# Register work of TensorE in the edge stage of a graph attention layer: tile addresses lowered ahead of the waits, a bit taken by a remainder

## Chip, cores and metric

One core of a Trainium2 chip runs the whole kernel in one launch. The metric is device microseconds from the start to the end of the execution.

## What is computed

The layer attends over the edges of a graph with 6250 nodes of 512 features (8 heads of 64) and 106,250 directed edges (each of 50,000 random pairs both ways, and one loop per node), sorted by destination:

```python
Q = (x @ Wq).reshape(N, H, d); K = (x @ Wk).reshape(N, H, d); V = (x @ Wv).reshape(N, H, d)
score = einsum('ehd,ehd->eh', K[src], Q[dst]) / sqrt(d)
score = exp(clip(score, -5.0, 5.0))[..., None]
wV = segment_sum(V[src] * score, dst, N)
Z = segment_sum(score, dst, N)
h = x + (wV / (Z + 1e-06)).reshape(N, D)
h = (h - mean(h, 0)) * rsqrt(var(h, 0) + 1e-05) * bn_gamma + bn_beta
return layernorm(x + h)
```

## The kernel before, in words

The program has three stages. `project` computes Q, K and V for 49 tiles of 128 nodes and stores them in HBM, K and V side by side. `attend` is the edge stage, about 1500 of the 2111 us, in which the change lies. `normalise` finishes the layer.

In the edge stage the sorted edges are cut into visits of 128 edges that belong to one tile of nodes. Two visits make a pair, and the stage walks over 440 pairs. Their buffers form a ring of 8 (`RING`): POOL fetches the rows of K and V of a pair into slot s of `kv` while seven others are at work. Each engine runs the same skeleton, `pipeline`: a few steps written out ahead, a hardware loop whose body holds 8 pairs (53 rounds), and a few steps behind. The order inside an engine is the order in which `step` is written; the engines meet at semaphores, one per slot of the ring for most.

For one pair q the engines do this:
- POOL issues two indirect DMAs (L747), one per visit, that gather 128 rows of K and V each. They wait until the slot's sums are done (`s_seg`). In every second pair it also weighs one head (L710).
- TensorE copies the rows of Q to the edges: a matmul of a one-hot matrix (`mm_sb`) with the tile of Q in `q_tile`, 2 visits × 2 halves = 4 matmuls into `q_ps` (L915). There is one `q_ps`, so the first of them waits until VectorE has multiplied the pair before (`s_mul`); the last raises `s_qx`.
- VectorE multiplies the gathered K by `q_ps` (L791), reduces it to 8 scores a row (L802), clips (L795), and weighs a part of the heads (L710). ScalarE takes the exponential (L856) and weighs 4 heads of each visit in 8 instructions (L842).
- TensorE adds the weighed rows into the sums of their nodes: 4 matmuls (8 passes in the trace) with the one-hot matrix the other way round, into one of two halves of `acc`, by the parity of the tile (L940). They wait for the weighing (`s_v`) and for the half to be emptied (`s_evict`); the last raises `s_seg`.
- In every second pair TensorE also makes the one-hot matrices of two later pairs (L925, L927), and ScalarE copies them to `mm_sb` (L852). Where a tile of nodes ends, ScalarE evicts its half of `acc` (L836, L838).

TensorE's order within a step is: q_ps of pair q + 1, the masks of q + 4 in even steps, the sums of q − 2.

Which tile a visit belongs to is data, so that TensorE and ScalarE follow it in registers. `follow` loads a mask of 16 bits per round; `bit(k)` says whether visit k starts a new tile. TensorE keeps the tile numbers of 8 visits (`tile_regs`, written at L907 and read at L932), and works out from them the parity that selects the half of `q_tile` (L915) and of `acc` (L940), and the values that `s_q` (Q's tile is loaded) and `s_evict` are compared with.
Of the kernel before, what the change touches and what calls it, by code (L numbers as in the profile page):

```python
# [25 lines left out]
F32R = mybir.dt.float32r  # L26
# [6 lines left out]
N_NODES, DIM, HEADS = 6250, 512, 8  # L33
D_HEAD = DIM // HEADS
N_EDGES = 106250
TILES = -(-N_NODES // P)
# [28 lines left out]
HALF = AGG // 2  # L65
# [9 lines left out]
def wait(eng, sem, value):  # L75

    if not (isinstance(value, int) and value <= 0):
        eng.wait_ge(sem, value)
# [547 lines left out]
def attend(nc, block, kv_d, q_d, lb_d, nb_d, xb_d, tabs, agg, rz, kv, first, x_first, s_first, s_slots, soft):  # L626
    lb, nb, q_tile, zeros, less, eps = first
    src_t, bits_row, cnt_row, ident = tabs
    with ExitStack() as ctx:
# [3 lines left out]
        def ps(name, shape, dt):  # L633
            return ctx.enter_context(nc.psum_tensor(name, shape, dt))
# [11 lines left out]
        acc = ps("acc", [P, 2, 2 * DIM], F32)  # L646
# [11 lines left out]
        s_nb, s_q = soft["s_nb"], soft["s_q"]  # L658
        s_qx, s_evc, s_evict = (soft[n] for n in ("s_qx", "s_evc", "s_evict"))
# [4 lines left out]
        def pipeline(eng, step, head):  # L664

            for q in range(-LOOKAHEAD, RING):
                step(q, q % RING, 1 + q // RING)
            with nc.Fori(1, ROUNDS - 1, engines=[eng.engine], head_slot={eng.engine: head}) as i:
                for s in range(RING):
                    step(i * RING + s, s, i + 1)  # L670
            for q in range((ROUNDS - 1) * RING, PAIRS + LAG):
                step(q, q % RING, q // RING + 1)

        def there(q):
            return not isinstance(q, int) or 0 <= q < PAIRS

        def at(s, fills, ahead):

            return (s + ahead) % RING, fills + (s + ahead) // RING

        def follow(eng, tiles):
            now, before = eng.alloc_register("mask_now"), eng.alloc_register("mask_before")
            regs = [eng.alloc_register(f"tile_{n}") for n in range(tiles)]
            for r in (now, *regs):
                eng.reg_mov(r, 0)

            def fetch(mask):
                eng.reg_mov(before, now)
                if not isinstance(mask, int) or mask < MASKS:
                    eng.reg_load(now, bits_row[0:1, bass.ds(mask, 1)])  # L690

            def bit(k, earlier=False):
                mask = eng.snap(before if earlier else now, min_val=0, max_val=2 ** VBODY - 1)
                return (mask >> k) & 1
            fetch(0)
            return regs, fetch, bit

        def one_hot(s, u, by_node):

            n = 2 * (s % 2) + u  # L700
            return mm_sb[:, s // 2, by_node, n * P:(n + 1) * P]
# [10 lines left out]
        @block.sync  # L712
        def _(sp):
            def load(t):
                sp.dma_start(q_tile[:, bass.ds(t % 2, 1), :].rearrange("p a n -> p (a n)"),
                             q_d[bass.ds(t * P, P), :]).then_inc(s_q, 16)

            sp.wait_ge(soft["s_tb"], 48)
            sp.wait_ge(soft["s_qa"], 16 * (TILES // 2 + 1))
            sp.wait_ge(soft["s_qb"], 16 * (TILES // 2))  # L720
            with sp.Fori(2, TILES) as t:
                used = sp.value_load(cnt_row[0:1, bass.ds(t - 2, 1)], min_val=1, max_val=VISITS)
                wait_apart(sp, s_qx, (used + 1) >> 1)
                sp.wait_ge(s_q, 16 * t)
                load(t)
            for t in range(FIRST_X):
                sp.dma_start(x_first[:, t, :], xb_d[t * P:(t + 1) * P, :]).then_inc(s_first, 16)
            for s in range(X_SLOTS):
                t = FIRST_X + 4 * s
                sp.wait_ge(s_seg[s], (PAIRS - 1 - s) // RING + 1)  # L730
                sp.dma_start(x_in_kv(kv, t, 4).rearrange("p (t n) -> p t n", n=DIM),
                             xb_d[t * P:(t + 4) * P, :].rearrange("(t p) n -> p t n", p=P)).then_inc(s_slots, 16)
# [147 lines left out]
        @block.tensor  # L880
        def _(pe):
            PLACES = RING
            pe.wait_ge(soft["s_visit"], 4)
            tile_regs, fetch, bit = follow(pe, PLACES)

            pe.wait_ge(soft["s_kc"], TILES // 2 + 3)
            def clear():

                pe.wait_ge(soft["s_split"], 2 * TILES)  # L890
                pe.wait_ge(soft["s_mem"], 1)
                for par in range(2):
                    for n in range(DIM - HALF, DIM + HALF, HALF // 2):
                        pe.matmul(acc[:, par, n:n + HALF // 2], zeros[:, 0:P], zeros[:, :], start=True,
                                  stop=True)
            pe.wait_ge(s_nb, 16)

            def step(q, s, fills):
                a, b, c = q + 4, q + 1, q - 2
                (sa, fa), (sb_, fb), (sc, fc) = at(s, fills, 4), at(s, fills, 1), at(s, fills, -2)  # L900
                if there(b):
                    tiles = []
                    for u in range(2):
                        v = 2 * sb_ + u
                        tile = pe.snap(pe.snap(tile_regs[(v - 1) % PLACES], min_val=0, max_val=TILES - 1)
                                       + bit(2 * s + u), min_val=0, max_val=TILES - 1)
                        pe.reg_mov(tile_regs[v % PLACES], tile)  # L907
                        tiles.append(tile)
                    multiplied = fills if isinstance(fills, int) else pe.to_reg(fills)
                    pe.wait_ge(s_mm[sb_ // 2], fb)  # L910
                    pe.wait_ge(s_q, 16 * (tiles[1] + 1))
                    for u in range(2):
                        for n in range(2):
                            part_q = q_tile[:, bass.ds(tiles[u] % 2, 1), n * DIM:(n + 1) * DIM].bitcast(F32R)
                            last = pe.matmul(q_ps[:, u, :], one_hot(sb_, u, 1), part_q, start=(n == 0),  # L915
                                             stop=(n == 1))
                            if u == n == 0 and there(q):
                                last._wait_ge(s_mul[s], multiplied)
                    last.then_inc(s_qx, 1)
                if s % 2 == 0 and there(a):  # L920
                    pe.wait_ge(s_lb[sa // LB_PAIRS], 16 * fa)
                    m1, f1 = at(s, fills, 2)
                    wait(pe, s_mm[m1 // 2], f1)
                    for n in range(4):
                        pe.matmul(mm_ps[:, 0, n * P:(n + 1) * P], lb[:, sa + n // 2, n % 2 * P:(n % 2 + 1) * P],  # L925
                                  nb[:, :], start=True, stop=True)
                    pe.matmul(mm_ps[:, 1, :], nb[:, :], lb[:, sa:sa + 2, :], start=True,  # L927
                              stop=True).then_inc(s_t[sa // 2], 1)
                if isinstance(q, int) and q == 0:
                    clear()  # L930
                if there(c):
                    tiles = [pe.snap(tile_regs[(2 * sc + u) % PLACES], min_val=0, max_val=TILES - 1)  # L932
                             for u in range(2)]
                    pe.wait_ge(s_v[sc], (2 if sc % 2 else 3) * fc)
                    pe.wait_ge(s_evict, tiles[1] + 1)
                    for u in range(2):
                        par = tiles[u] % 2
                        m = one_hot(sc, u, 0).bitcast(F32)
                        for n in range(2):
                            last = pe.matmul(acc[:, bass.ds(par, 1), DIM - (1 - n) * HALF:DIM + n * HALF], m,  # L940
                                             kv[:, sc, u, DIM + n * HALF:DIM + (n + 1) * HALF],
                                             start=False, stop=True, skip_group_check=True)
                    last.then_inc(s_seg[sc], 1)
                if s == RING - 1:
                    fetch(q // RING + 2 if isinstance(q, int) else fills + 1)
            pipeline(pe, step, PE_HEAD)

# [431 lines left out]
```

## Time and profile before

| | |
|---|---|
| median of 3 runs | 2119.94 us (2118.71 to 2123.97) |
| the profiled execution, its own time | 2113.25 us |
| its span, first to last instruction | 2111.5 us |
| granted TensorE clock, mean | 0.99 of full speed |
| TensorE matmuls busy | 1918.3 us |
| VectorE busy | 1696.9 us |
| ScalarE busy | 1377.7 us |
| POOL busy | 1249.1 us |
| share of the chain that ended last: PE, DVE, issue | 70%, 16%, 7% |

Busy times count work on data only; register steps, branches, semaphores and the issue of DMAs are not in them. PE is TensorE's matmuls, PEld its weight loads, which overlap them; a q behind an engine's name is its sequencer. The chain follows the work that ended last back to what released it. "Issue" is time in which an engine waited for nothing that the profile shows; "remote" is a releaser that the profile can't name. Ends of matmuls are modelled.

### The profile page before, as it was taken

The page shows a single profiled execution, that of the slowest core. Times are in us where ns is not written, and L with a number is a line of the kernel's source. Part 1 is how long each engine was busy: PE and PEld are TensorE (multiplying, and loading weights), DVE is VectorE, ACT ScalarE, POOL GpSimd, SP SyncE. Part 2 cuts the span into 40 slices and gives each one's busy share as a digit, 9 for nine tenths or more (in the row PEclk, how much of TensorE's full clock was granted, in tenths as well). Part 3 has the DMA queues.
Part 4 walks back from the last instruction along what each step waited for, and adds up shares of the span by engine and source line. Part 5 has one row for each costly group of instructions (what it writes and reads, how often), then busy time and mean ns, then how long its engine had stood idle before and what let it go on. Part 6 is the DMA issues. An engine that isn't in the chain of part 4 may idle for free.

```text
span 2111.5 us, 41623 instructions
## 1 busy us (share of the span) xinstructions
PE 1918.3 (91%) x7904; PEld 1351.1 (64%) x8014; DVE 1696.9 (80%) x2454; ACT 1377.7 (65%) x4602; POOL 1249.1 (59%) x1473
## 2 busy tenths in 40 slices
PE   7999999989998998998899899898899899899887
PEld 4555555547776776776677677676676677677433
DVE  6676655538888888888888888888888888888988
ACT  0001000018887887887888888788788788788866
POOL 0106663026666666666666666666666666666657
PEclk9999999999999999999999999999999999999999
DMA  4648886358998898888888989898899899889607
GB/s 172 176 147 299 293 301 237 143 206 300 315 326 291 304 322 307 313 305 309 306 307 305 325 315 311 301 314 300 296 321 309 294 317 320 307 300 331 225 0 289
DMA packets 184521, 589.09 MB, mean 279 GB/s; under 512 B 28480, under 2 KB 30240, under 8 KB 184480
## 3 DMA queue, kind: packets, MB, share of 16 engines
q0 software_dynamic: 135904, 465.14, 63.5%
q1 hardware_dynamic: 45120, 121.69, 16.2%
q10 hardware_dynamic: 3456, 1.78, 0.3%
q8 instruction: 18, 0.29, 0.1%
q14 instruction: 23, 0.19, 0.0%
HBM read 535.27 MB, written 78.91 MB: 291 GB/s over the span
## 4 chain that ended last, share of the span: by engine, by line
PE 70%; DVE 16%; issue 7%; another core or an unknown queue 2%; ACT 2%; DMA 1%; POOL 1%; SPq 0%; DVEq 0%; ACTq 0%; POOLq 0%
PE q_ps L915 26%; PE places L342 20%; PE acc L940 19%; DVE kv L791 11%; PE mm_ps L925 2%; DVE stats L1278 1%; DVE agg L1262 1%; ACT agg L1189 1%; DVE raw L802 1%; PE mm_ps L927 1%; DVE agg L1271 1%; PE places L402 1%; PE banks L1132 1%; DMA kv<-kv_d,idx 1%
## 5 line engine op out<-in xcount | busy, mean ns | idle before, releaser
L747 POOL DMA_INDIRECT kv<-kv_d,idx x880 | 891.9, 1014 | 548.9 <-issue 214.0
L842 ACT ACTIVATE kv<-kv 128x64 f32<-128x64 f32 x3520 | 888.9, 335 | 14.3
L940 PE MATMUL acc<-kv,mm_sb 128*128 128x260 f32 x3520 | 852.1, 385 | 11.9 <-issue 4.4
L940 PEld LDWEIGHTS acc<-kv,mm_sb 128*128 128x128 f32 x3520 | 672.8, 192 | 114.3 <-issue 10.7
L791 DVE TENSOR_TENSOR kv<-q_ps,kv 128x1024 f32<-128x1024 f32 x440 | 536.4, 1219 | 214.7 <-PE q_ps L915 161.1
L915 PE MATMUL q_ps<-q_tile,mm_sb 128*128 x1760 | 550.0, 434 | 146.0 <-DVE kv L791 114.7
L802 DVE TENSOR_REDUCE raw<-kv 128x16 f32<-128x1024 f32 x440 | 532.7, 1211 | 0.0
L915 PEld LDWEIGHTS q_ps<-q_tile,mm_sb 128*128 128x128 f32 x1760 | 316.9, 190 | 285.3 <-DVE kv L791 193.6
L852 ACT ACTIVATE mm_sb<-mm_ps,less 128x1024 fp32r<-128x1024 f32 x220 | 241.5, 1098 | 66.2 <-remote 60.1
L710 DVE TENSOR_TENSOR kv<-kv 128x384 f32<-128x384 f32 (+1 forms) x440 | 271.8, 618 | 0.0
L856 ACT ACTIVATE kv<-raw 128x16 f32<-128x16 f32 x440 | 92.0, 209 | 197.9 <-DVE raw L795 181.8
L342 PE MATMUL places<-t_sb,s_sb 128*128 128x512 f32 (+1 forms) x552 | 185.5, 486 | 0.0
L435 ACT COPY p<-places 128x768 f32<-128x768 f32 x23 | 18.4, 799 | 247.8 <-PE places L342 247.8
L342 PEld LDWEIGHTS places<-t_sb,s_sb 128*128 128x128 f32 x552 | 104.8, 190 | 73.6 <-issue 66.5
L710 POOL TENSOR_TENSOR kv<-kv 128x128 f32<-128x128 f32 x220 | 91.7, 417 | 60.6 <-ACT kv L856 48.5
L342 PE MATMUL places<-w_sb,x_sb 128*128 128x512 f32 (+1 forms) x368 | 126.2, 486 | 0.0
L795 DVE TENSOR_SCALAR raw<-raw 128x16 f32<-128x16 f32 x440 | 103.6, 235 | 0.0
L342 PEld LDWEIGHTS places<-w_sb,x_sb 128*128 128x128 f32 x368 | 69.8, 190 | 49.1 <-issue 44.5
L925 PEld LDWEIGHTS mm_ps<-nb,lb 128*128 128x128 bf16 x880 | 50.5, 99 | 63.2 <-issue 63.2
L925 PE MATMUL mm_ps<-nb,lb 128*128 128x128 bf16 x880 | 88.6, 224 | 1.5 <-issue 1.5
L590 DVE TENSOR_TENSOR u<-places,p 128x768 f32<-128x768 f32 x23 | 22.0, 957 | 78.3 <-PE places L342 78.3
L440 ACT COPY kv_a<-places 128x256 f32<-128x256 f32 x23 | 8.6, 372 | 98.0 <-PE places L342 55.8
(171 smaller groups left out, 1354.1 us busy)
## 6 DMA issues: line engine op xcount, KB each, us to landing
q_tile<-q_d SPq DMA_DIRECT2D x49, 512.0 KB
kv<-kv_d,idx POOLq DMA_INDIRECT x880
kv_d<-kv_a SPq DMA_DIRECT2D x25, 512.0 KB
xb<-in_x POOLq DMA_DIRECT2D x49, 256.0 KB, 4.2
xb_d<-xb POOLq DMA_DIRECT2D x49, 256.0 KB, 3.7
out_rows<-agg SPq DMA_DIRECT2D x49, 256.0 KB, 2.1
x_sb<-in_xT SPq DMA_DIRECT2D x24, 512.0 KB, 8.1
q_d<-q_a SPq DMA_DIRECT2D x24, 512.0 KB
```

What stands on the lines that cost most here:

```text
L342: last = pe.matmul(out[:, cols], left[:, c, :], right[:, c, cols], start=fresh and c == 0, stop=c == DEEP - 1, skip_group_check=True)
L710: return eng.tensor_tensor(v, v, w, ALU.mult)
L747: pool.indirect_dma_start(kv[:, s, u, 0:2 * DIM], None, kv_d, bass.IndirectOffsetOnAxis(idx[:, s, u:u + 1], 0), bounds_check=N_NODES - 1, ...
L791: dve.tensor_tensor(k, q_ps[:, :, :], k, ALU.mult).then_inc(s_mul[s], 1)
L795: dve.tensor_scalar(raw[:, s1, :, :], raw[:, s1, :, :], -5.0, 5.0, ALU.max, ALU.min).then_inc(s_clip[s1], 1)
L802: dve.tensor_reduce(raw[:, s, :, :], heads(kv[:, s, :, 0:DIM]), AX.X, ALU.add).then_inc(s_red[s], 1)
L842: return act.activation(v, v, ACT.Copy, scale=kv[:, s, u, 2 * DIM + h:2 * DIM + h + 1])
L852: act.activation(mm_sb[:, sa // 2, :, :], mm_ps[:, :, :], ACT.Relu, bias=less[:, 0:1]).then_inc(s_mm[sa // 2], 1)
L856: act.activation(kv[:, s, :, 2 * DIM:KVW], raw[:, s, :, :], ACT.Exp).then_inc(s_exp[s], 1)
L915: last = pe.matmul(q_ps[:, u, :], one_hot(sb_, u, 1), part_q, start=(n == 0), stop=(n == 1))
L925: pe.matmul(mm_ps[:, 0, n * P:(n + 1) * P], lb[:, sa + n // 2, n % 2 * P:(n % 2 + 1) * P], nb[:, :], start=True, stop=True)
L940: last = pe.matmul(acc[:, bass.ds(par, 1), DIM - (1 - n) * HALF:DIM + n * HALF], m, kv[:, sc, u, DIM + n * HALF:DIM + (n + 1) * HALF], sta ...
```

## The change

`bit` takes the lowest bit by a remainder, where it used an AND. In the q part TensorE works out the value for `s_q`, builds the four views of `q_tile` and has them lowered to register addresses (`lower_ap`) ahead of the two waits; the matmuls then use the finished views. In the part with the sums it does the same with the four views of `acc` and the value for `s_evict`. No matmul, tile or semaphore is added or taken away, and no other engine's code is touched, except that ScalarE's `bit` is the same function. Lines behind L907 move down by 5, those behind L932 by 9 (L915 is L920, L940 is L949).

```diff
--- before.py
+++ after.py
@@ -691,7 +691,7 @@
 
             def bit(k, earlier=False):
                 mask = eng.snap(before if earlier else now, min_val=0, max_val=2 ** VBODY - 1)
-                return (mask >> k) & 1
+                return (mask >> k) % 2
             fetch(0)
             return regs, fetch, bit
 
@@ -907,11 +907,16 @@
                         pe.reg_mov(tile_regs[v % PLACES], tile)
                         tiles.append(tile)
                     multiplied = fills if isinstance(fills, int) else pe.to_reg(fills)
+                    loaded = pe.snap(16 * (tiles[1] + 1), min_val=16, max_val=16 * TILES)
+                    parts = [q_tile[:, bass.ds(tiles[u] % 2, 1), n * DIM:(n + 1) * DIM].bitcast(F32R)
+                             for u in range(2) for n in range(2)]
+                    for part_q in parts:
+                        pe.lower_ap(part_q)
                     pe.wait_ge(s_mm[sb_ // 2], fb)
-                    pe.wait_ge(s_q, 16 * (tiles[1] + 1))
+                    pe.wait_ge(s_q, loaded)
                     for u in range(2):
                         for n in range(2):
-                            part_q = q_tile[:, bass.ds(tiles[u] % 2, 1), n * DIM:(n + 1) * DIM].bitcast(F32R)
+                            part_q = parts[2 * u + n]
                             last = pe.matmul(q_ps[:, u, :], one_hot(sb_, u, 1), part_q, start=(n == 0),
                                              stop=(n == 1))
                             if u == n == 0 and there(q):
@@ -931,13 +936,17 @@
                 if there(c):
                     tiles = [pe.snap(tile_regs[(2 * sc + u) % PLACES], min_val=0, max_val=TILES - 1)
                              for u in range(2)]
+                    sums = [acc[:, bass.ds(tiles[u] % 2, 1), DIM - (1 - n) * HALF:DIM + n * HALF]
+                            for u in range(2) for n in range(2)]
+                    emptied = pe.snap(tiles[1] + 1, min_val=1, max_val=TILES)
+                    for part in sums:
+                        pe.lower_ap(part)
                     pe.wait_ge(s_v[sc], (2 if sc % 2 else 3) * fc)
-                    pe.wait_ge(s_evict, tiles[1] + 1)
+                    pe.wait_ge(s_evict, emptied)
                     for u in range(2):
-                        par = tiles[u] % 2
                         m = one_hot(sc, u, 0).bitcast(F32)
                         for n in range(2):
-                            last = pe.matmul(acc[:, bass.ds(par, 1), DIM - (1 - n) * HALF:DIM + n * HALF], m,
+                            last = pe.matmul(sums[2 * u + n], m,
                                              kv[:, sc, u, DIM + n * HALF:DIM + (n + 1) * HALF],
                                              start=False, stop=True, skip_group_check=True)
                     last.then_inc(s_seg[sc], 1)
```

The q part of one pair on TensorE, before. Each row is one instruction; a row that names no operation on a tile is register work, and the brackets give the semaphores it waits for (`s_mul2` is that of slot 2):

```order
L905 ISA
L907 REGISTER_ALU
L907 ISA
L907 REGISTER_ALU
L907 ISA
L911 ISA [waits s_mm1]
L915 ISA [waits s_q]
L915 MATMUL q_ps<-q_tile,mm_sb 128x512 [waits s_mul2]
L915 ISA
L915 MATMUL q_ps<-q_tile,mm_sb 128x512
```

(The last two rows come twice more.) The same place now:

```order
L905 ISA
L907 ISA
L914 ISA x2
L916 ISA [waits s_mm1]
L920 MATMUL q_ps<-q_tile,mm_sb 128x512 [waits s_q,s_mul2]
L920 MATMUL q_ps<-q_tile,mm_sb 128x512 x3
```

Of ten register instructions five are left. Nothing stands between the matmuls, two bundles of addresses (L914) stand ahead of them, and the wait for `s_q` is a condition of the first matmul.

The sums of one pair on TensorE, right ahead of that place, before:

```order
L932 ISA
L935 REGISTER_ALU [waits s_v7]
L940 ISA [waits s_evict]
L940 MATMUL acc<-kv,mm_sb 128x260
L940 ISA
L940 MATMUL acc<-kv,mm_sb 128x260
L940 ISA
L940 MATMUL acc<-kv,mm_sb 128x260
L940 ISA
L940 MATMUL acc<-kv,mm_sb 128x260
```

and now:

```order
L937 ISA
L943 ISA x2
L945 REGISTER_ALU [waits s_v7]
L949 MATMUL acc<-kv,mm_sb 128x260 [waits s_evict]
L949 MATMUL acc<-kv,mm_sb 128x260 x3
```

Six register instructions have become four. The bundle that stood between the wait for `s_v` and the first matmul is ahead of that wait; a register step that carries the wait itself is still there.

## Rows read from the trace of the kernel before

**Rows 1.** The page, part 1: engine, busy us (share of the span), instructions.
```profile
PE 1918.3 (91%) x7904; PEld 1351.1 (64%) x8014; DVE 1696.9 (80%) x2454; ACT 1377.7 (65%) x4602; POOL 1249.1 (59%) x1473
```

**Rows 2.** Page, part 5: group, count | busy us, mean ns | idle before.
```profile
L940 PE MATMUL acc<-kv,mm_sb 128*128 128x260 f32 x3520 | 852.1, 385 | 11.9 <-issue 4.4
```

**Rows 3.** Waits, whole span: waiter <- releaser: us in total, times, longest.
```profile
POOL kv L747 <- remote: 212.7, 174, 1.7
...
DVE kv L791 <- PE q_ps L915: 161.1, 192, 1.6
...
PEld q_ps L915 <- issue: 39.8, 27, 3.1
PE q_ps L915 <- issue: 29.4, 20, 2.7
...
PEld acc L940 <- issue: 10.7, 19, 1.4
```

**Rows 4.** The chain of waits from 1707.8 to 1721.3: start us, us, what.
```profile
1707.87 1.24 DVE kv L791
...
1709.15 1.20 PE q_ps L915 x4
...
1712.56 1.89 PE q_ps L915 x4
...
1714.55 1.24 DVE kv L791
```

**Rows 5.** Timeline, 1709.8 to 1722.6: start us, us, operation [idle before].
```profile
1710.65 1.92 PE L940 MATMUL acc<-kv,mm_sb 128*128 128x260 f32 x8
...
1712.21 1.28 PE L915 MATMUL q_ps<-q_tile,mm_sb 128*128 x4
...
1712.48 0.99 POOL L747 DMA_INDIRECT kv<-kv_d,idx  x1 [0.30 <-issue]
1712.49 1.21 DVE L802 TENSOR_REDUCE raw<-kv 128x16 f32<-128x1024 f32 x1
...
1714.55 1.23 DVE L791 TENSOR_TENSOR kv<-q_ps,kv 128x1024 f32<-128x1024 f32 x1 [0.85 <-PE q_ps L915]
1715.17 1.03 POOL L747 DMA_INDIRECT kv<-kv_d,idx  x1 [1.26 <-remote]
...
1717.37 1.21 DVE L791 TENSOR_TENSOR kv<-q_ps,kv 128x1024 f32<-128x1024 f32 x1
```

**Rows 6.** Timeline from 1154 to 1160, where POOL left a hole.
```profile
1155.76 1.21 DVE L791 TENSOR_TENSOR kv<-q_ps,kv 128x1024 f32<-128x1024 f32 x1
...
1158.69 1.21 DVE L791 TENSOR_TENSOR kv<-q_ps,kv 128x1024 f32<-128x1024 f32 x1
```

**Rows 7.** TensorE's register steps of L935 and L940 at 1002.6: duration ns min/median/max.
```profile
L935 PEldq ALU_OP  x1: 36/36/36, 1002.6 to 1002.6; - x1
...
L940 PEldq FUSED_REGOPS  x1: 102/102/102, 1002.7 to 1002.7; - x1
```

**Rows 8.** Timeline from 999.9 to 1003.2: the weighings and the weight load behind them.
```profile
1000.55 2.02 ACT L842 ACTIVATE kv<-kv 128x64 f32<-128x64 f32 x8
...
1002.86 0.52 PEld L940 LDWEIGHTS acc<-kv,mm_sb 128*128 128x128 f32 x3 [0.81 <-issue]
```

**Rows 9.** Register steps of the whole span by line: count, ns min/median/max.
```profile
L907 PEldq ALU_OP  x880: 3/34/727, 461.9 to 1956.4; - x176
L907 PEldq FUSED_REGOPS  x880: 3/104/727, 462.0 to 1956.5; - x176
...
L915 PEldq FUSED_REGOPS  x1760: 3/56/724, 462.5 to 1957.8; - x196
...
L940 PEldq FUSED_REGOPS  x1760: 3/51/482, 473.8 to 1965.4; - x196
```

**Rows 10.** Register bundles of L915, 1713.9 to 1715.9: ns, first and last start.
```profile
L915 PEldq FUSED_REGOPS  x2: 13/32/51, 1714.3 to 1715.8; - x2
```

**Rows 11.** The same from 1717.5 to 1719.0.
```profile
L915 PEldq FUSED_REGOPS  x4: 51/72/105, 1717.9 to 1718.9; - x4
```

## The prediction, made before the changed kernel ran

> **What bounds the kernel now.** I read the page's busy times first: TensorE is busy for 91% of the span and VectorE for 80% [rows 1], so no engine can be named from shares alone. The costliest groups come next: beside a matmul group stands the idle time just ahead of it, and the sums by node (L940) are 852.1 us of work with 11.9 us of idle [rows 2]. So their group hardly ever stands still for its own reasons. The waits tell more. Inside the edge stage two large ones belong together: POOL's gathers wait 212.7 us for a "remote", 174 times, and VectorE's multiplication (L791) waits 161.1 us, 192 times, for the q_ps matmuls (L915) [rows 3]. TensorE in turn may not overwrite q_ps before that multiplication is over, so the two form a loop that all 440 pairs of visits run through.
>
> The chain of waits over two pairs shows it as a cycle of 6.68 us, from the multiplication at 1707.87 to that at 1714.55: multiplication 1.24, q_ps matmuls 1.20, mask matmuls, sums, and then q_ps matmuls again, which the chain prices at 1.89 us [rows 4]. The timeline of the same place gives that last group 1.28 us: it begins at 1712.21 and is over by 1713.49, VectorE's reduce by 1713.70, yet the multiplication begins at 1714.55, 0.85 us after VectorE was free and 1.06 us after the matmuls' end [rows 5]. In the same instant something else is late: POOL's gather of 1715.17 waited 1.26 us for a "remote" though the sums that it needs ended at 1712.57 (10.65 + 1.92) [rows 5]. Both late signals follow the fourth of four back-to-back gathers (1712.48). Where POOL leaves a hole between gathers, the multiplication begins without any gap: 1155.76 and 1158.69, a step of 2.93 us against 3.34 in the cycle [rows 6]. So I read the bound as this: half of the pairs lose some 0.8 us because TensorE's updates arrive late while POOL gathers, and in a pair where they do not, VectorE sets the pace.
>
> **The change, part by part.** Counted in the two orders, TensorE's sequencer runs 16 register instructions a pair before (10 for the q part, 6 for the sums) and 9 after. All are in the sequencer and none in the array, so each costs time only where the array or a waiter stands still for it.
>
> *The sums.* Before, behind the wait for the weighed rows stood the register move that carries it (36 ns), a bundle (102 ns) and a step to the first weight load [rows 7]. The one clear place: ScalarE's eight weighings end at 1002.57 (1000.55 + 2.02), the weight load begins at 1002.86 [rows 8]. Of these 0.29 us the move stays (L945 still carries the wait), the bundle goes, and with it I take half of the remaining 0.15 us of steps: 0.10 + 0.06 = 0.16 us. It is gained only where TensorE had nothing else to do: the waits name 19 such starts, 10.7 us in all [rows 3]. 19 × 0.16 = **3.0 us**. The other 421 starts follow matmuls without a hole, and what hides the bundle there is the matmuls ahead of it.
>
> *The bundles between the matmuls of a group* (3 for q_ps, 3 for the sums, medians 56 and 51 ns [rows 9]) go away. The chain has the four q_ps matmuls in 1.20 us [rows 4], 0.30 us each, five times a bundle; the cover is the array itself: 0. A page's rule bears on this. The Trainium skill, "Perfetto Trace Analysis", Sequencer Loop and Tensor Engine Instruction, has a waiting matmul pushed into a queue, with the sequencer free to go on. By that rule the register work behind a waiting matmul was hidden before as well, and the whole edit would be worth 0. The trace disagrees in one place: the bundle ahead of the first q_ps matmul ran at 1714.3 and the next only at 1715.8, when the multiplication that the matmul waits for was over [rows 10]. So the sequencer stood with the matmul, and I keep the 3.0 us, which the rule does not give.
>
> *The q part.* Here the change moves work to a dearer place: three address bundles that stood between matmuls now stand ahead of the first (3 × 56 ns), and a bit costs a remainder in place of an AND of its own. The first bundle of L940, which takes the parity of the tile by a remainder, was 102 ns long [rows 7], against a median of 51 over all four of its bundles, and an AND is a step of 34 ns [rows 9]; so + 51 ns twice, less two ANDs: 168 + 102 − 68 = **+ 0.20 us** from the last matmul of the sums to the wait for the multiplication. The cover: where TensorE had waited, the sequencer stood from 1714.3 to 1715.8, 1.4 us of slack [rows 10]. Where TensorE runs on without a hole, the sequencer comes to its wait near 1718.0, and the multiplication ends at 1718.58 (1717.37 + 1.21): 0.5 us [rows 5, 11]. Both are over 0.20, so 0. The bounds: at best the pair loses all the idle time put on "issue" ahead of this group's weight loads, 39.8 us in 27 times [rows 3]; at worst the 0.20 us stand bare in each second pair, 220 × 0.20 = 44 us. I take 0, by the two covers.
>
> *The waits on s_q and s_evict* now compare with a register worked out ahead. Neither of the two stands among TensorE's larger waits, so 0. The wait on s_q becomes a condition of the matmul, with nothing of TensorE's queued behind it that did not stand behind it before. *ScalarE* loses three of four ALU steps at L870, which at the 36 ns of TensorE's [rows 7] are 0.11 us a pair beside eight weighings of 2.02 us; ScalarE is at 65% and not in the chain: 0. VectorE, POOL, SyncE and every DMA stay as they are.
>
> **Sum**: 2113.25 us of the profiled run − 3.0 = 2110.25. That run lies 6.7 us below the median of 2119.94, so the forecast for the median is **2117 us**, less than 0.3% (6.4 us) away from no change, and that is about what a measurement of this kernel can tell from none.
>
> **Rivals.** *Faster: the late signals are TensorE's own doing.* If the q_ps update comes late because TensorE's sequencer is busy with register steps, fewer of them make it earlier. For: only signals of TensorE and POOL are late, and the steps have outliers of 727 ns against medians of 104 and less [rows 9]. Against: POOL's share in it, and the undisturbed pairs with the same register work and no gap [rows 6]. Prices: in proportion to the instructions, 7/16 of VectorE's 161.1 us = 70 us, to 2050. If only the idle time put on "issue" shrinks by that share, 29.4 us ahead of q_ps, with all 11.9 us ahead of the sums [rows 2, 3], it is 41.3 × 7/16 = 18 us, to 2102. There is also a threshold: the sums end 0.09 us after the fourth gather's start (1712.57 against 1712.48 [rows 5]), and a little less delay might let their signal through in time. I give the mild form 0.25 and the large one 0.10.
>
> The Trainium skill, "Perfetto Trace Analysis", Tensor Engine Instruction, says that the end of a matmul in the profile is an estimate and that its signal goes out when PSUM has acknowledged. By that rule alone the 1.06 us would be matmuls still running, TensorE would be the bound, and a change in its sequencer would give 0. The undisturbed pairs, whose multiplication starts with no gap behind the same matmuls, speak against it; it would alter nothing in the forecast.
>
> *Slower: the longer row of register steps ahead of the first q_ps matmul meets its wait too late.* It decides from a cover of less than 0.20 us. For: there is idle time put on "issue" ahead of this group's weight loads, 27 times, and ahead of its matmuls, 20 times [rows 3]; there the sequencer already comes last, and each would lose the full 0.20: at most 47 × 0.20 = 9 us, to 2129. If the cover of 0.5 us that I read at one place is missing in many of the pairs without a hole, up to 44 us, to 2164. Against: both covers [rows 5, 10, 11]. I give it 0.20, most of it near 2129.
>
> *The change doesn't do what it says.* In part this is so: the value that s_q is compared with is still made by the step that waits for s_mm, and L945 still follows s_v. What is left behind the wait is 36 ns; had the bundle stayed too, the 3.0 us would be 0 and the forecast 2120, which is inside it.
>
> **How the numbers follow.** Forecast (no difference to be seen) 0.45; faster 0.35; slower 0.20. The range reaches down to 2085, half of the large form's 70 us, and up to 2136, past the 9 us of the slower case with some of its tail; left out are the rest of the large form and the far slower end. The forecast's own range is 2114 to 2123.
>
> **What would show it.** In the profile after: no register bundle between the matmuls of a group; weight loads of the sums 0.13 us, not 0.29, after the last weighing where they wait for it; VectorE still waiting about 160 us for q_ps in some 190 times; the two-pair cycle still 6.7 us; L870 with about 440 ALU steps in place of 1705. If VectorE's wait for q_ps or POOL's for the remote falls by tens of us, the late signals hung on TensorE's sequencer and I am wrong; if the idle time put on "issue" ahead of q_ps grows, the slower rival is at work.

## The result: 0.9% slower, and the profile after

| | before | changed |
|---|---|---|
| median of 6 runs each | 2119.32 us | 2135.01 us (2131.33 to 2145.51) |
| ratio, 95% interval | | 1.0089 [1.0063, 1.0114] |
| profiled execution, own time | 2113.25 us | 2132.71 us |
| its span | 2111.5 us | 2130.9 us |
| granted TensorE clock, mean | 0.990 | 0.984 |

The forecast was no difference, 2117 us, in a range of its own of 2114 to 2123; the measured 2135 lies above it. The sign was that of the rival to which I had given 0.20. The three groups that matter, from the page of the changed kernel (L949 is the sums, L920 the q_ps matmuls):

```profile
L949 PE MATMUL acc<-kv,mm_sb 128*128 128x260 f32 x3520 | 856.1, 387 | 12.9 <-issue 6.5
...
L791 DVE TENSOR_TENSOR kv<-q_ps,kv 128x1024 f32<-128x1024 f32 x440 | 536.5, 1219 | 226.0 <-PE q_ps L920 118.4
L920 PE MATMUL q_ps<-q_tile,mm_sb 128*128 x1760 | 554.9, 437 | 156.0 <-DVE kv L791 114.3
```

VectorE's idle time ahead of its multiplication, 214.7 us before, is 226.0, so 11 of the 19 us between the two spans stand at this one place. By stage, 13.6 of the 19 us lie in the edge stage (1495.1 us from the first to the last multiplication before, 1508.7 after). Another 5.8 us lie ahead of it, where the two kernels have the same code: the stage starts at 463.9 and at 469.7 us, and at 463.5 to 468.4 in the traces of the experiments. The waits of the whole span split VectorE's idle time:

```profile
POOL kv L747 <- remote: 161.7, 126, 1.8
DVE kv L791 <- PE q_ps L920: 118.4, 148, 1.8
...
DVE kv L791 <- remote: 98.8, 40, 3.9
...
PEld q_ps L920 <- issue: 56.0, 38, 3.7
...
PEld acc L949 <- issue: 10.9, 18, 1.3
```

Against [rows 3] VectorE's wait for q_ps fell from 161.1 us to 118.4. A row that I had seen in the waits before and left out of my argument, VectorE's wait for a "remote", rose from 44.9 us in 19 cases to 98.8 in 40. I had taken it for gathered rows that come late. In the case below it is not. It is from the timeline of the changed kernel from 945 to 952:

```profile
945.83 1.28 PE L920 MATMUL q_ps<-q_tile,mm_sb 128*128 x4
...
946.16 0.99 POOL L747 DMA_INDIRECT kv<-kv_d,idx  x1 [0.31 <-issue]
...
947.18 0.41 POOL L710 TENSOR_TENSOR kv<-kv 128x128 f32<-128x128 f32 x1
948.03 1.03 POOL L747 DMA_INDIRECT kv<-kv_d,idx  x1 [0.43 <-issue]
949.36 1.00 POOL L747 DMA_INDIRECT kv<-kv_d,idx  x1 [0.30 <-issue]
950.26 1.23 DVE L791 TENSOR_TENSOR kv<-q_ps,kv 128x1024 f32<-128x1024 f32 x1 [2.93 <-remote]
```

and in its chain of waits:

```profile
946.11 1.22 DVE raw L802
947.33 2.84 another core or an unknown queue
950.17 0.03 issue
950.20 0.02 DVEq L789
```

L789 is VectorE's wait for `s_qx`, the signal of the q_ps matmuls. They were over at 947.11, and the event of `s_qx` stands at 950.17, 0.03 us ahead of L789. The last event of this pair's gathers in the trace stands at 942.84 (it holds 18 of their 32), and the multiplication began 0.04 us behind L789, so it did not wait for them. So this is the late signal of [rows 4, 5] again, 3 us long in place of 1. In [rows 5] POOL waited 1.26 us between its fourth and its fifth gather, and the signal came in that pause. Here POOL weighed a head, went on 0.43 us after that, and the signal came 0.80 us into the second of two more gathers. So the picture of a signal that comes in a pause of POOL fits the short delays and not the long ones. Of the `s_qx` events that the trace of before holds, 182 come 0.3 to 1.2 us behind their matmuls, and 180 of these between two gathers; 24 come later than 1.2 us, and 14 of these fall inside a gather (in the changed kernel 24 of 47). Counted over all multiplications of the edge stage, idle time of 0.3 to 1.2 us ahead of one fell from 152.0 us in 186 cases to 112.1 in 140, and idle time over 1.2 us rose from 58.9 us in 29 to 107.7 in 46.

Behind some of these long gaps the granted clock falls to its lower level, 1.2 GHz, here for some 3 us:

```profile
1693.50:1697.40 3.90, 2.47 (x12) 1.74 (x10) 0.40 (x1) 3.15 (x11) 2.89 (x4) 1.00 0.87 270
1697.50:1700.50 3.00, 1.74 (x4) 1.16 (x4) 2.88 (x4) 1.64 (x7) 2.03 (x2) 0.65 0.64 202
1700.50:1701.70 1.20, 0.98 (x6) 0.97 (x7) 0.75 (x1) 0.59 (x3) 0.90 (x1) 0.50 0.81 311
```

(From the windows: stretch, its length, busy time of PE, PEld, DVE, ACT and POOL with their instructions, granted clock, DMA share, GB/s.) By the clock records of the traces it happened behind 13 of the 46 gaps of over 1.2 us, and behind 8 of 29 before. In the edge stage TensorE stood at the lower level for 51.2 us, where it had been 30.7. What that adds to the time, apart from the idle time, isn't separated here.

What I had forecast of the register work is there. A place where the sums wait for ScalarE's weighing, to be held against [rows 8]:

```profile
963.32 1.77 ACT L842 ACTIVATE kv<-kv 128x64 f32<-128x64 f32 x7
...
965.22 0.52 PEld L949 LDWEIGHTS acc<-kv,mm_sb 128*128 128x128 f32 x3 [0.57 <-issue]
```

965.22 − (963.32 + 1.77) = 0.13 us, where it was 0.29. And the bundles:

```profile
L905 PEldq FUSED_REGOPS  x387: 236/242/262, 467.4 to 1974.8; - x194
...
L907 PEldq FUSED_REGOPS  x440: 243/274/287, 467.7 to 1975.1; - x147
...
L943 PEldq FUSED_REGOPS  x880: 64/92/117, 478.0 to 1982.6; - x176
```

### The profile page after: what moved, and what is told of

Same layout as the page of the kernel before. It is cut to its first block, busy times and chain, and to the rows that moved or that the text cites. A ratio compares the mean times of both kernels' runs of the same rounds, so it can differ in the third digit from the quotient of the medians.

```text
span 2130.9 us, 37662 instructions
## 1 busy us (share of the span) xinstructions
PE 1923.6 (90%) x7904; PEld 1359.2 (64%) x8014; DVE 1699.2 (80%) x2454; ACT 1378.6 (65%) x4602; POOL 1255.1 (59%) x1473
## 4 chain that ended last, share of the span: by engine, by line
PE 67%; DVE 21%; issue 5%; another core or an unknown queue 3%; DMA 2%; ACT 1%; POOL 0%; DVEq 0%; SPq 0%; ACTq 0%; POOLq 0%
PE q_ps L920 23%; PE acc L949 22%; PE places L342 18%; DVE kv L791 11%; DVE raw L802 3%; PE mm_ps L930 2%; DVE stats L1287 1%; DVE agg L1271 1%; DMA kv_d<-kv_a 1%; PE mm_ps L932 1%; DVE agg L1280 1%; PE places L402 1%; PE banks L1141 1%; DMA kv<-kv_d,idx 1%
## 5 line engine op out<-in xcount | busy, mean ns | idle before, releaser
L949 PE MATMUL acc<-kv,mm_sb 128*128 128x260 f32 x3520 | 856.1, 387 | 12.9 <-issue 6.5
L949 PEld LDWEIGHTS acc<-kv,mm_sb 128*128 128x128 f32 x3520 | 676.2, 193 | 116.3 <-issue 10.9
L791 DVE TENSOR_TENSOR kv<-q_ps,kv 128x1024 f32<-128x1024 f32 x440 | 536.5, 1219 | 226.0 <-PE q_ps L920 118.4
L920 PE MATMUL q_ps<-q_tile,mm_sb 128*128 x1760 | 554.9, 437 | 156.0 <-DVE kv L791 114.3
L920 PEld LDWEIGHTS q_ps<-q_tile,mm_sb 128*128 128x128 f32 x1760 | 319.8, 191 | 288.0 <-DVE kv L791 177.4
L795 DVE TENSOR_SCALAR raw<-raw 128x16 f32<-128x16 f32 x440 | 92.0, 209 | 0.0
```

Source lines behind the costliest of these rows:

```text
L791: dve.tensor_tensor(k, q_ps[:, :, :], k, ALU.mult).then_inc(s_mul[s], 1)
L795: dve.tensor_scalar(raw[:, s1, :, :], raw[:, s1, :, :], -5.0, 5.0, ALU.max, ALU.min).then_inc(s_clip[s1], 1)
L949: last = pe.matmul(sums[2 * u + n], m, kv[:, sc, u, DIM + n * HALF:DIM + (n + 1) * HALF], start=False, stop=True, skip_group_check=True)
```

## Experiments

"Before" in the results below is always the kernel before, run in turn with the experiment on the same chip.

### Which part of the change

**e1**, the remainder alone:

```diff
-                return (mask >> k) & 1
+                return (mask >> k) % 2
```

> The kernel before with the remainder alone in place of the AND. In the changed kernel the bundles of the q part that hold the bits are 242 and 274 ns long, against 74 and 104 before; but no q_ps group there started later than its wait and TensorE allowed. Theory A (late signals): the whole change lost 15.7 us because VectorE's idle time of over 1.2 us ahead of a multiplication grew from 58.9 us in 29 cases to 107.7 in 46, while that of 0.3 to 1.2 us fell from 152 to 112; which part of the change shifts it is open, and this one alone should stay near before, 2119, within 6 us, unless the remainder is the part. Theory B (sequencer time): what costs is the longer work for a bit, so this kernel has most of the loss: 2130 or more, with idle time ahead of the q_ps matmuls that no wait explains.

2129.17 us beside 2113.77, ratio 1.0055 [1.0034, 1.0077]: most of the loss, just below the 2130 of theory B.

**e2**, the q part's lowering alone (the first hunk behind `bit` in the diff of the change, with the AND kept; the rows left out put the finished views and `loaded` in their places):

```diff
+                    loaded = pe.snap(16 * (tiles[1] + 1), min_val=16, max_val=16 * TILES)
+                    parts = [...]
+                    for part_q in parts:
+                        pe.lower_ap(part_q)
...
```

> The kernel before with only the q part's views and the value for s_q worked out ahead of the waits, and the AND kept. Theory A: the four q_ps matmuls go out back to back the moment the multiplication is over, the phase between TensorE and POOL's gathers shifts, and most of the loss is here: 2128 to 2138. Theory B: without the remainders of the bits the row is shorter by some 0.3 us, so the loss is mostly gone: 2115 to 2124.

2112.56 us beside 2113.77, 0.9989 [0.9973, 1.0006]: below the ranges of both theories.

**e3**, the lowering for the sums alone:

```diff
+                    sums = [...]
+                    emptied = pe.snap(tiles[1] + 1, min_val=1, max_val=TILES)
+                    for part in sums:
+                        pe.lower_ap(part)
...
```

> The kernel before with only the views of acc and the value for s_evict worked out ahead of the waits. By my prediction's own sum this is where 3.0 us are gained: 2112 to 2119. Theory A: a shift of the sums against the gathers by a few tens of ns can go either way, up to 15 us. Theory B: no row is lengthened ahead of q_ps; 2116 to 2119.

2113.15 us beside 2113.77, 0.9999 [0.9984, 1.0014].

**e4**, both lowerings, the AND kept (e2 and e3 together):

```diff
-                return (mask >> k) % 2
+                return (mask >> k) & 1
```

(against the changed kernel)

> Both lowerings, with the AND kept: the change without its remainder. Theory A: as slow as the changed kernel, 2130 to 2138, with over 40 waits of more than 1.2 us ahead of a multiplication. Theory B: the remainder was the cost, so 2112 to 2120.

2113.83 us beside 2113.77, 1.0000 [0.9985, 1.0015].

So beside a kernel before at 2114 the lowerings neither gain nor lose, and the remainder alone loses most of what the change lost. It looked like theory B, sequencer time, but the traces say no. From TensorE's first step of the bits (L905) to the end of its wait for Q's tile the row takes 0.86 us before and 1.13 in e4, which is no slower; in e1, which is, it takes 0.72 (medians of 387). Its bundles are longer, but the two ANDs, each a step of its own with a gap behind it, are gone. The waits of e1 show the same shift as those of the changed kernel:

```profile
DVE kv L791 <- PE q_ps L915: 143.2, 171, 2.2
...
DVE kv L791 <- remote: 76.7, 33, 4.1
```

and e4's are those of before:

```profile
DVE kv L791 <- PE q_ps L920: 164.5, 191, 3.2
...
DVE kv L791 <- remote: 45.2, 18, 4.5
```

### Which engine's remainder

`follow` serves both engines; ScalarE uses the bit to decide on an eviction.

**e5**, on TensorE alone:

```diff
-                return (mask >> k) & 1
+                return (mask >> k) % 2 if tiles > 1 else (mask >> k) & 1
```

> The remainder on TensorE alone, ScalarE keeps the AND. The remainder alone lost 15.4 us, though TensorE's register row from its first step to the wait for Q's tile is shorter with it (0.72 us against 0.86 before, and 1.13 with both lowerings, which lose nothing). Theory B1 (TensorE): long bundles of 226 and 171 ns do harm there whatever the row's length: 2125 to 2132. Theory B2 (ScalarE): the bit is ScalarE's too, where it decides the eviction and its bundle went from 120 to 268 ns; then this kernel is at 2110 to 2118, as before.

**e6**, on ScalarE alone:

```diff
-                return (mask >> k) & 1
+                return (mask >> k) % 2 if tiles == 1 else (mask >> k) & 1
```

> The remainder on ScalarE alone, TensorE keeps the AND. Theory B1 (TensorE): 2110 to 2118, as before. Theory B2 (ScalarE): the whole loss is here, 2125 to 2132. If neither of the two shows it and only both together do, it is a matter of the two engines' phase.

1908.75 us (0.9989 [0.9979, 0.9998]) and 1911.77 us (1.0002 [0.9992, 1.0011]), both beside a kernel before at **1911.44 us**, not at 2114. In this series of runs (e5 and e6 shared a chip and its kernel before) there were no late signals, and the theories could not be told apart: VectorE's idle time ahead of its multiplications was 7.2 and 9.0 us. The same happened in later series, and three chips (3, 8 and 9) showed both conditions, so it does not belong to a chip alone. Each result below is therefore read by its own kernel before.

**e7**, the changed kernel again, **e8** and **e9**, e5 and e6 again:

> The changed kernel once more. In the last two kernels' runs everything, the kernel before too, took 1911 us in place of 2114, and the trace shows why: not one late signal of TensorE, VectorE idle 7 to 9 us ahead of its multiplications in place of 212. Theory A (the loss is in the late signals alone): where the kernel before runs at 1911, the changed kernel is within 3 us of it; where it runs at 2114, it is at 2127 to 2140. Theory B (work of the sequencers): the same loss of 12 to 20 us wherever it runs.

> The remainder on TensorE alone. Beside a kernel before at 2114: Theory B1 (TensorE's remainder carries the loss) 2125 to 2132, theory B2 (ScalarE's) 2110 to 2118. Beside one at 1911: both say no difference over 3 us.

> The remainder on ScalarE alone. Beside a kernel before at 2114: theory B1 2110 to 2118, theory B2 2125 to 2132. Beside one at 1911: no difference over 3 us.

Beside 1911.90 us: e7 1906.81 us, 0.9972 [0.9962, 0.9982]; e8 1908.01, 0.9980 [0.9969, 0.9992]; e9 1911.58, 0.9993 [0.9982, 1.0005]. **Without late signals the change is 5 us faster**, and the remainder on TensorE alone (e8) gains 4. Theory B, the same loss wherever the kernel runs, is refuted. Of theory A what holds is that the loss comes only with late signals; its "within 3 us" was missed, as I had not foreseen a gain, and so was e8's. The gain shows in the waits of TensorE's weight loads for the multiplication. e9, with TensorE's steps as before:

```profile
PEld q_ps L915 <- DVE kv L791: 23.8, 77, 2.9
```

e8:

```profile
PEld q_ps L915 <- DVE kv L791: 12.6, 24, 3.1
```

and e7:

```profile
PEld q_ps L920 <- DVE kv L791: 8.3, 18, 2.1
```

53 waits fewer in e8 and 59 in e7, and there are 53 rounds. At a round's end TensorE loads the next mask and branches before it works out the next bits. e9 there, in its timeline:

```profile
1054.27 1.23 DVE L791 TENSOR_TENSOR kv<-q_ps,kv 128x1024 f32<-128x1024 f32 x1
...
1055.71 1.19 PE L915 MATMUL q_ps<-q_tile,mm_sb 128*128 x4
```

The multiplication ends at 1055.50 and q_ps begins 0.21 us later. With the remainder on TensorE (e8) the same place reads:

```profile
1053.29 1.23 DVE L791 TENSOR_TENSOR kv<-q_ps,kv 128x1024 f32<-128x1024 f32 x1
...
1054.58 1.29 PE L915 MATMUL q_ps<-q_tile,mm_sb 128*128 x4
```

0.06 us. Of the eight pairs of a round, this one has a median from multiplication to q_ps of 0.213 us in e9 and 0.067 in e8; in the other seven the two are alike within 0.05. The difference, 0.15 us in 53 rounds, is 7.7 us; the time fell by 3.9 in e8.

The changed kernel closes the same gap although its row is longer (1.08 us). In e8 and e9 address bundles stand between the matmuls of the sums, and in all rounds TensorE's sequencer reaches the mask's load only when two or three of the eight passes have begun. In e7 it reaches it ahead of all eight, during the q_ps matmuls. So the lowering for the sums might bring the gain by itself. No run shows it: e2 to e4 ran with late signals alone.

**e10**, the remainder on TensorE alone once more:

> The remainder on TensorE alone, for a comparison beside a kernel before at 2114, the condition in which the changed kernel lost. There theory B1 (TensorE's remainder shifts the late signals) says 2125 to 2132, theory B2 (ScalarE's does) 2110 to 2118. Beside a kernel before at 1911 it should be 2 to 4 us faster once more, and settles nothing on that.

This time beside 2113.14 us: 2113.01, 1.0009 [0.9988, 1.0030]. TensorE's remainder alone doesn't carry the loss.

**e11**, the changed kernel with ScalarE's AND kept (the line of e5), and **e12**, e6 again:

> The changed kernel with the AND kept on ScalarE, the remainder on TensorE alone. TensorE's remainder by itself lost nothing beside a kernel before at 2113 (ratio 1.0009). Theory B2 (ScalarE's remainder carries the loss): beside a kernel before at 2114 this one is at 2108 to 2118, 15 us or more under the changed kernel; beside one at 1911 it keeps the gain of the changed kernel, 4 to 6 us. Theory B3 (any short timing shift does it, ScalarE has no part of its own): near 2128 beside 2114.

> The remainder on ScalarE alone. Theory B2: beside a kernel before at 2114, 2125 to 2132, with over 40 waits of more than 1.2 us ahead of a multiplication. Theory B4 (only both engines' remainders together do it): 2110 to 2118. Beside a kernel before at 1911: no difference over 3 us.

Beside 1910.88 us: 1907.24 (0.9974 [0.9964, 0.9984]) and 1912.22 (1.0002 [0.9992, 1.0012]). The gain without late signals needs no remainder on ScalarE (3.6 us here, a little under the 4 to 6 expected).

**e13** is e6 again and **e14** e1 again:

> The remainder on ScalarE alone, for a comparison beside a kernel before at 2114. Theory B2 (ScalarE's remainder carries the loss): 2124 to 2132, ratio 1.004 to 1.008. Theory B4 (both engines' remainders together): 2108 to 2118. Beside a kernel before at 1911 it says no difference, and this stays open.

> The remainder on both engines, as in the first run that showed the loss alone (2129.2 beside 2113.8). Beside a kernel before at 2114 it must show it again, 2122 to 2132, or the loss was one of that session. Beside one at 1911: 2 to 4 us faster, as with the remainder on TensorE alone.

Beside 1912.27 us: 1911.69 (1.0002 [0.9993, 1.0012]) and 1907.90 (0.9982 [0.9969, 0.9995]). The kernel that had lost 0.55% gains 0.18% here. Whether it would lose 0.55% again with late signals was not measured.

**e15**, e6 again; **e16**, e11 again:

> As for the run before: the remainder on ScalarE alone. Beside a kernel before at 2114, theory B2 says 2124 to 2132 and theory B4 (both engines' remainders together) 2108 to 2118; beside one at 1911, no difference.

> The changed kernel with the AND kept on ScalarE. Beside a kernel before at 2114: theory B2 (ScalarE's remainder is needed for the loss) 2108 to 2118; theory B3 (any shift of TensorE's steps by more than its remainder alone, the lowerings too, does it) 2125 or more. Beside one at 1911: 4 to 6 us faster, as it was.

1911.57 beside 1911.91 (1.0002 [0.9990, 1.0014]), and 1906.46 beside 1911.24 (0.9976 [0.9964, 0.9987]).

**e17**, e6 again:

> The remainder on ScalarE alone, once more in the hope of a kernel before at 2114: theory B2 2124 to 2132, theory B4 (both engines' together) 2108 to 2118. Beside one at 1911 no difference, and the split of the loss between the engines stays open.

2107.02 beside 2099.73 us, **1.0050 [1.0027, 1.0073]**. With late signals, the remainder on ScalarE alone loses as much as both do in e1, in the one such series that it had. That both remainders are needed (theory B4) is refuted. Its waits:

```profile
DVE kv L791 <- PE q_ps L915: 121.3, 156, 2.5
...
DVE kv L791 <- remote: 84.5, 34, 3.4
```

against those of e10, TensorE alone:

```profile
DVE kv L791 <- PE q_ps L915: 158.5, 188, 3.2
...
DVE kv L791 <- remote: 51.4, 21, 3.9
```

The waits show how the delays changed and not where the 0.5% went. The executions that were profiled took the same time in the two series (2112.32 and 2112.01 us), with VectorE idle ahead of its multiplications for 208.7 and 209.8 us, and of e17's own kernel before, 13 us faster than e10's, there is no trace.

**e18**, e11 again, with late signals:

> The changed kernel with the AND kept on ScalarE. ScalarE's remainder alone has now lost 0.5% beside a kernel before at 2100. Theory B2: beside a kernel before at 2090 to 2115 this one is within 0.25% of it. Theory B3 (the lowerings with TensorE's remainder lose too): 0.4% or more slower. Beside one at 1911: 4 to 6 us faster.

2125.13 beside 2118.85 us, 1.0026 [1.0000, 1.0051]; its runs spread from 2112.62 to 2139.95. It is neither within the 0.25% of theory B2 nor at the 0.4% of B3, and its VectorE waited 84.6 us in 36 cases for a "remote", in a profiled execution that was the slowest of the ten, 15 us above their median. So to keep the AND on ScalarE does not surely save the changed kernel. That the whole of its loss is ScalarE's is not shown.

## Why the prediction was wrong

- **The sums**, − 3.0 us: the step was right in size at its place (0.29 to 0.13 us, as forecast) and nothing of it is seen in the time: e3 measured 0.9999, with an interval of 0.15% to each side, about the 3.0 us themselves.
- **The bundles between matmuls**, 0: right. The 1.20 us of a q_ps group in [rows 4] is 1.19 to 1.20 after, where it starts on an idle TensorE.
- **The q part**, + 0.20 us hidden: the row grew by 0.22 (0.86 to 1.08 us), and the covers of 0.5 and 1.4 us held: e4, with 1.13, loses nothing. The working was wrong inside. A bit's remainder costs more than my 51 ns (bundles of 242 and 274 ns for [rows 9]' 104 and less), and an AND costs more than its 34, as the gap behind a separate step goes with it. I also read the cover at two places and took it for all. With late signals that did no harm: at a round's end q_ps follows the multiplication as closely as elsewhere. Without them there is no cover at each round's end, and closing that gap is a gain of 3 to 5 us. The bounds that I gave, 39.8 us down and 44 up, were far too wide for it.
- **The slower rival** had the right sign and named time (2129) by the wrong mechanism. Its test was idle time put on "issue" ahead of q_ps, and that did grow, from 39.8 to 56.0 us. It proves nothing: in e17, where TensorE's steps are those of before, it is 55.4 us. In the trace of the changed kernel TensorE's row was the last thing that a q_ps group waited for, by over 0.06 us, once in 440; before it was six times.
- **ScalarE**, 0 us: **this is the step that failed.** "ScalarE is at 65% and not in the chain: 0." Without late signals that is so: four comparisons gave 1.0002 and one 0.9993. With them the same edit on ScalarE alone cost 0.50%, in one series, and with the AND kept on ScalarE the changed kernel lost 0.26% in its series, where the whole change had lost 0.89% in another. I also counted only the ALU steps that go away and not the bundle that grows, from 120 to 268 ns (L866). I had costed the step by its own time, beside a loop that closes to within 0.1 us between two engines ([rows 5]: sums end 0.09 us after the gather starts).
- **The faster rival** was half right: fewer waits for q_ps, 161.1 to 118.4 us. I had named the threshold, and not that a signal late by 1 us could turn into one late by 3; that the threshold is what was crossed isn't shown. VectorE's 44.9 us on "remote" held examples of such signals and I did not read them. I was also wrong that POOL's own signals are late: of the events that the traces hold only TensorE's are, and POOL's gather of 1715.17 in [rows 5] waited for a signal of TensorE.

How ScalarE's steps reach TensorE's signals is open, and what makes up the changed kernel's other 0.3 to 0.4% is too: its parts on TensorE cost nothing one by one (e4, e10), and e18, which has them together, has an interval from 0 to 0.5%. In the repeated two-pair cycle of each trace, ScalarE's weighings start within 3 ns of where they did. Its bundle at L866 is 268 ns in place of 120, its branch comes 0.05 us sooner, and POOL's first gather starts 10 to 28 ns later behind the multiplication (642 ns in e1, 642 in e17 and 660 in the changed kernel, against 632 before and 630 in e10; medians). Fewer of the 219 two-pair steps keep the pattern, a length of 6.55 to 6.75 us: 155 before, 151 in e10, 120 in e1, 102 in the changed kernel and 59 in e17, where 39 more are 6.45 to 6.55 us long (4 at most in the others). In e18, with ScalarE's steps as before, the gather starts at 640 ns and 110 keep it. The order of loss follows that gather's delay only roughly, and no run moved the gather alone.

## What to carry to other kernels

Read what stands behind a "remote" before the argument: compare the wait's end with the semaphores that the instruction waits for, one by one. If a stage's period is set by a signal that comes late and not by work, then the cost of an edit there can't be summed from durations, and even one on an engine off the chain may move it; measure it, and in more than one series. Covers are to be read at the loop's end too, where a load and a branch stand ahead of the row.

## What the runs showed of the hardware

The same kernel before took 2089 to 2126 us in some series of runs and 1906 to 1919 in others, and the difference lies in the edge stage: from first to last multiplication 1495.1 us in the trace of before, 1285.4 in e7, with VectorE idle ahead of them 212.2 and 6.7 us. The windows of e7 (columns as above):

```profile
600.00:1700.00 1100.00, 1093.46 (x5365) 898.92 (x5458) 1097.37 (x1507) 1045.37 (x3662) 901.40 (x1035) 1.00 0.97 360
```

TensorE and VectorE are busy nearly all the time (1093 and 1097 of 1100 us), and the DMA engines move 360 GB/s, against 309 before from 600 to 1800 us. In the slower series only TensorE's signals are seen to come late: of the 268 events of `s_qx` that the trace of before holds in the edge stage, 206 stand over 0.3 us behind their matmuls, and none of the events of VectorE, ScalarE or POOL that it holds does. In e7 none of 439 is late. The traces of the slower series hold only part of the events of every engine, and of the gathers' semaphores 7326 of 14,080 before, but 14,073 in e7. Something about these signals differs from series to series; what it is no run here tells.
